# The adjacency build of a four-layer graph network, its three-lap loop written out on four engines

## The chip, the cores and the metric

The kernel runs on one core of one Trainium2 chip. The metric is the device time of one execution in microseconds. The kernel before takes 2465.7 us, the median of three runs (2464.94 to 2465.91).

## The reference

A graph of 6,250 nodes with 128 features and 206,250 directed edges (each of 100,000 random edges both ways, and a loop at each node) passes through four layers. Each layer normalizes the rows, applies a ReLU, sums over the edges and adds the result to `x`:

```
h = relu(layernorm(x)); x = x + segment_sum(edge_weight * (sigmoid(h @ Wg + bg) * (h @ W0))[dst], src)   # layer 0
h = relu(layernorm(x)); x = x + segment_sum(h[src], dst) @ W1.T + b1                                     # layer 1
h = relu(layernorm(x)); x = x + [h, segment_sum([h[src], h[dst]] @ Wm + bm)] @ Wu + bu                   # layer 2
h = relu(layernorm(x)); x = x + relu(batchnorm(D^-1 A (B^-1 A^T (h @ W3)) + b3))                          # layer 3
```

The same edge list serves all layers, so the sums over edges are products with a dense matrix of edge counts (layers 1 to 3) and of edge weights (layer 0).

## The kernel before

The 6,250 nodes lie in 49 tiles of 128. The program has three stages.

The **preparation** (up to about 100 us) loads the edges, groups them by destination, and computes layer 0's gated rows `G`.

The **build** (about 100 to 1190 us) makes the matrices, one destination tile at a time; a tile takes some 21.7 us. Four engines work on it, each with its own instruction stream, joined by semaphores alone:

- VectorE (DVE; `build` at L1059 with `hots` at L1030): for each of 8 steps h of a tile it makes one-hot rows (L1043, L1044), multiplies one set by the edge weights (L1046, which raises `hot_ready`), and adds a finished partial sum into `X` (`add_some`, L1057, which raises `added`).
- TensorE (PE; `build` at L747): for each h it waits for `hot_ready` (L751), then does two half windows (`half_windows`, L711): 12 matmuls each of one-hot rows into PSUM (L732 to L734), one matmul that takes the rounded high part away (L709), and in some of them two turns of a block (L725). Then it does a share of layer 0's sum for a pair of tiles built earlier (`sum_some`, L701 to L703). The sum of a pair starts in the first step of the next odd tile, behind the waits of `loaded` (L737), which hold until the pair's weight matrices have been turned by the DMA engines and have landed in `wt`.
- ScalarE (ACT; `build` at L1331) rounds the high parts out of PSUM (L1348, `hi_done`), the low parts (L1329, `lo_done`) and the turned blocks (L1358).
- SyncE's queue (SP; `hand_on`, L468) waits until the sums have freed a home in `wt` (`sum_made`, L477 to L480), then for `hi_done`; it loads the gated rows `g_in` (L486), issues two DMA transposes `wt<-stage` (L489), stores the counts (L493), waits for `lo_done`, loads `g_in` again and issues two more transposes. Every two tiles it loads the next edge group `meta` (L475).

So there is a ring: PE's sums of the pair of tiles before wait for transposes of that pair, and SP's transposes wait for what ACT and PE made of the current tile. Two tiles are one **pair** in the text below: an even tile and the odd one behind it.

The **passes** (about 1235 to 2440 us) multiply the counts with the rows, four times over all 49 tiles (L804), with the counts streamed from HBM. Each engine runs each pass as a loop as well.

All these loops come from one helper, `tiles_loop` (L145). It writes out the first 13 tiles (0 to 12), then opens a hardware loop of three laps with twelve tiles in its body (tiles 13 to 24, 25 to 36, 37 to 48), then writes out a drain of `lag` more steps. In the loop the tile number `j` is a register expression, so a wait such as `pe.wait_ge(s("hot_ready"), j * TILE_HOTS + (h + 1))` needs register arithmetic ahead of it; in the written-out part it is a constant. The build calls it on four engines, at L496 (SP), L764 (PE), L1087 (DVE) and L1363 (ACT).

Of the kernel before, what the change touches and what calls it, by code (L numbers as in the profile page):

```python
# [21 lines left out]
TILES = -(-NODES // P)  # L22
# [22 lines left out]
CHUNKS = -(-EDGES // P)  # L45
PADDED = CHUNKS * P
PLANES = 4
CODE = 1.0 / 64.0
RECORD = 5 * ALIGN // 2
X_PARTS = (range(0, 13), range(13, 25), range(25, 37), range(37, TILES))  # L50
# [6 lines left out]
SLOTS = 6  # L57
LAP = 2 * SLOTS
# [83 lines left out]
    return (c // 2 + 2) % (SLOTS // 2)  # L142


def tiles_loop(eng, body, lag):  # L145

    peel = LAP + 1
    for j in range(peel):
        body(j, 0, j)
    with eng.Fori(0, (TILES - peel) // LAP) as k:  # L150
        for u in range(LAP):
            body(k * LAP + (peel + u), k * (LAP // SLOTS), peel + u)
    for j in range(TILES, TILES + lag):
        body(j, 0, j)


# [45 lines left out]
def gnn_kernel(nc, x, src, dst, edge_weight, w0, wg0, bg0, w1, b1, wm, bm, wu, bu, hyper, w3, b3, gamma, beta, out):  # L202
    ctx = ExitStack()
    with ctx:
        sems = {}

        def s(name):
            if name not in sems:
                sems[name] = ctx.enter_context(nc.semaphore(name))
            return sems[name]  # L210
# [3 lines left out]
        def at(name, shape, dt, offset):  # L214
            size = int(np.prod(shape[1:])) * ESIZE[dt]
            return nc.alloc_sbuf_tensor_at(name, shape, dt, offset=offset), offset + -(-size // 32) * 32
# [73 lines left out]
        src_low, _ = at("src_low", [P, RUN], I32, o)  # L290
        pre, o = at("pre", [P, 2, BATCH, PLANES, P], F16, o)
        src_high, _ = at("src_high", [P, RUN], I32, o)
        turned, o = at("turned", [P, 2, BATCH, PLANES, P], F16, o)
        w_run, o = at("w_run", [P, RUN], F32, o)
# [92 lines left out]
        def _(sp):  # L387
# [63 lines left out]
            def layers(general):  # L451
# [41 lines left out]
                    sp.dma_start(two_tiles(j), stage[:, b, 0:FULL].rearrange("p (i a) d -> p i (a d)", a=2)).then_inc(s(f"stored{b}"), 16)  # L493
                    turn(1, "lo_done", f"lo_turned{b}")

                tiles_loop(sp, hand_on, 0)  # L496
                for a in range(WEIGHTS):
                    first = FULL + a * TILES + TURN_FIRST
                    sp.dma_start_transpose(wt[:, home(TILES - 1, 1), a, len(BY_DMA[1]):len(HALF_TILES[1])],
# [143 lines left out]
        def _(pe):  # L643
# [43 lines left out]
            def layers(general):  # L687
# [73 lines left out]
                if general:  # L761
                    general_sum(0)
                else:
                    tiles_loop(pe, build, 0)  # L764
                    for u in (HALVES - 2, HALVES - 1):
                        pe.wait_ge(s("hi_done"), (TILES - 1) * HALVES + u + 1)
                        take_high(0, TILES - 1, u)
                    for n in (GROUPS - 2, GROUPS - 1):
                        for b in range(1 + (n < GROUPS - 1)):
                            loaded(n, b)  # L770
                        for g in range(SUMS):
                            sum_some(n, n, g, n < GROUPS - 1)
# [79 lines left out]
        def _(dve):  # L852
# [10 lines left out]
            v.tensor_scalar(before[:], diff[:], 0, None, ALU.is_gt)  # L863
            v.tensor_scalar(basef[:], basei[:], CODE, None, ALU.mult)
            v.memset(ones[:], 1.0).then_inc(s("consts"), 1)
            dve.wait_ge(s("iotas"), 5)
            v.tensor_scalar(iota_c[:], iota_c[:], CODE, None, ALU.mult)
            dve.wait_ge(s("consts"), 1)
# [91 lines left out]
            def edge_keys(m, at_step):  # L960
# [10 lines left out]
                if at_step == 1:  # L971
                    v.tensor_copy(to(3), plane(2))
                    for i, g in enumerate(lot):
                        last = v.tensor_scalar(to(1)[:, i], rec[:, g, :, 24:40].bitcast(F32), CODE, basef[:, g:g + 1], ALU.mult, ALU.add)
                    last.then_inc(s("pre"), 1)
# [51 lines left out]
            def layers(general):  # L1027
# [46 lines left out]
                if general:  # L1074
                    dve.wait_ge(s("g_iotas"), 1)
                    v.memset(rows_all[:], 0.0).then_inc(s("g_prep"), 1)
                    dve.wait_ge(s("g_prep"), 1)
                    v.tensor_scalar(rows_all[:, :, 0:P], H0[:], 1.0 / H_UP, None, ALU.mult).then_inc(s("g_rows_all"), 1)
                    general_sum(0)
                    v.tensor_tensor(X[:], X[:], acc[:, :, 0:P], ALU.add).then_inc(s("g_prep"), 1)  # L1080
                    dve.wait_ge(s("g_prep"), 2)
                    for j in range(TILES):
                        v.bn_stats(stats[:, j], X[:, j])
                else:
                    dve.wait_ge(s("g_parts"), SET)
                    v.tensor_scalar(w_h[:], w_h[:], 1.0 / LOW, None, ALU.mult)
                    tiles_loop(dve, build, 0)  # L1087
                    for g in range(SUMS - 2, SUMS):
                        add_some(GROUPS - 3, g)
                    for n in (GROUPS - 2, GROUPS - 1):  # L1090
                        for g in range(SUMS):
                            add_some(n, g)
                            if n == GROUPS - 1 and g:
                                row_stats(g - 1)
                    row_stats(SUMS - 1)
# [39 lines left out]
                for ph in (1, 2, 3, 4):  # L1135
# [112 lines left out]
                    if ph == 1 and not general:  # L1248
                        degrees(Chain(dve, s("dve_b"), c1.n), LOW)

            branch(dve, layers)


# [22 lines left out]
        def _(act):  # L1276
# [48 lines left out]
            def layers(general):  # L1325
# [34 lines left out]
                if not general:  # L1360
                    for b in range(2):
                        a.activation(stage[:, b, TILES], minus16[:], ACT.Copy, scale=0.0)
                    tiles_loop(act, build, 0)  # L1363
                    for u in (HALVES - 2, HALVES - 1):
                        act.wait_ge(s("low_left"), (TILES - 1) * HALVES + u + 1)
                        low_parts(0, TILES - 1, u)
# [93 lines left out]
```

## Time and profile before

| | before |
|---|---|
| runs, median (lowest to highest) | 2465.7 us (2464.94 to 2465.91) |
| the profiled execution: its time, its span | 2461.69 us, 2459.8 us |
| PE busy | 2293.2 us (93%) |
| PE weight loads busy | 2025.0 us (82%) |
| DVE busy | 1444.7 us (59%) |
| ACT busy | 1279.8 us (52%) |
| mean granted TensorE clock | 0.978 |
| bytes moved by DMA | 569.80 MB, 232 GB/s |
| code loads (queues of kind "instruction") | q8: 200 packets, 3.28 MB; q14: 84 packets, 0.68 MB |

The span is the time from the first to the last instruction of the profiled execution. Busy time is the sum over an engine's instructions; matmuls are pipelined, so a busy PE need not be at its peak. The profiled execution is 4.0 us shorter than the median of the runs. The packets of kind "instruction" are loads of program code into the engines' instruction stores.

### The profile page before, as it was taken

How to read it: one execution, taken by the hardware profiler on the slowest of the kernel's cores; microseconds unless marked ns; L12 is line 12 of the kernel's file. 1: busy time of each engine (PE TensorE's matmuls, PEld its weight loads, DVE VectorE, ACT ScalarE, POOL GpSimd, SP SyncE). 2: the span in 40 equal slices, each digit the busy share in tenths (PEclk: the TensorE clock that was granted, in tenths of full speed). 3: DMA queues.
4: the chain of work that ended last, by engine and by line, in shares of the span. 5: the costliest groups of instructions: out<-in, count | busy, mean ns of one | idle time of the engine just before them, and what ended most of it. 6: DMA issues, size and time to landing. Idle time of an engine off the chain costs nothing.

```text
span 2459.8 us, 72172 instructions
## 1 busy us (share of the span) xinstructions
PE 2293.2 (93%) x28669; PEld 2025.0 (82%) x28669; DVE 1444.7 (59%) x3422; ACT 1279.8 (52%) x2875; POOL 57.0 (2%) x57
## 2 busy tenths in 40 slices
PE   3689999999999989999889998999998999998997
PEld 3469898998899889988768887888887888887886
DVE  8779999998899988989643233234333111222223
ACT  3689999999899989989342222222221000011112
POOL 3500000000000000000000000000000000000000
PEclk9799999999999999999989999999999999999998
DMA  7799999999999999999989999999998999999997
GB/s 188 182 213 195 201 212 207 209 210 200 189 208 208 196 203 195 205 197 205 226 202 291 290 290 290 248 261 257 258 261 214 291 290 290 264 252 241 269 268 188
DMA packets 1528563, 569.80 MB, mean 232 GB/s; under 512 B 869815, under 2 KB 1526971, under 8 KB 1528152
## 3 DMA queue, kind: packets, MB, share of 16 engines
q1 hardware_dynamic: 1524709, 559.04, 104.0%
q0 software_dynamic: 1200, 4.10, 0.6%
q8 instruction: 200, 3.28, 0.5%
q10 hardware_dynamic: 2370, 2.71, 0.4%
q14 instruction: 84, 0.68, 0.1%
HBM read 257.85 MB, written 92.19 MB: 142 GB/s over the span
## 4 chain that ended last, share of the span: by engine, by line
PE 63%; SPq 16%; ACT 9%; DMA 5%; issue 4%; DVE 3%; POOLq 1%; another core or an unknown queue 0%; POOL 0%; DVEq 0%; ACTq 0%
PE ps L804 35%; SPq L542 8%; SPq L489 5%; ACT stage L1348 4%; PE ps L732 4%; ACT stage L1329 3%; PE ps L733 3%; PE ps L734 3%; PE ps L701 3%; PE ps L702 3%; PE ps L703 3%; PE ps L709 3%; DMA wt<-stage 3%; SPq L486 2%; PE ps L725 1%
## 5 line engine op out<-in xcount | busy, mean ns | idle before, releaser
L1348 ACT CAST stage<-ps 128x784 f16<-128x784 f32 x784 | 657.4, 838 | 18.0 <-PE ps L734 10.5
L804 PE MATMUL ps<-Ha,a_tiles 128*128 128x258 f16 x4606 | 523.9, 273 | 7.2 <-DVE Ha L1124 7.2
L732 PE MATMUL ps<-hot_c,hot_r 128*128 128x98 f16 x3136 | 502.7, 210 | 13.5 <-DVE hot_c L1046 10.4
L804 PEld LDWEIGHTS ps<-Ha,a_tiles 128*128 128x128 f16 x4606 | 449.9, 98 | 73.5 <-DVE Ha L1124 7.6
L733 PE MATMUL ps<-hot_c,hot_r 128*128 128x98 f16 x3136 | 500.4, 210 | 0.0
L734 PE MATMUL ps<-hot_c,hot_r 128*128 128x98 f16 x3136 | 498.8, 209 | 0.0
L701 PE MATMUL ps<-g_in,wt 128*128 128x128 f16 x2401 | 426.9, 220 | 29.2 <-DMA wt<-stage 20.1
L1329 ACT CAST stage<-ps 128x392 f16<-128x392 f32 x784 | 405.1, 517 | 43.4 <-PE ps L709 40.8
L703 PE MATMUL ps<-g_in,wt 128*128 128x128 f16 x2401 | 426.9, 220 | 0.0
L702 PE MATMUL ps<-g_in,wt 128*128 128x128 f16 x2401 | 426.9, 220 | 0.0
L1046 DVE TENSOR_TENSOR hot_c<-hot_c,meta 128x1568 f16<-128x1568 f16 x392 | 379.2, 967 | 0.0
L732 PEld LDWEIGHTS ps<-hot_c,hot_r 128*128 128x128 f16 x3136 | 307.3, 98 | 42.3 <-ACT stage L1329 21.8
L733 PEld LDWEIGHTS ps<-hot_c,hot_r 128*128 128x128 f16 x3136 | 308.2, 98 | 13.9 <-issue 1.1
L734 PEld LDWEIGHTS ps<-hot_c,hot_r 128*128 128x128 f16 x3136 | 308.3, 98 | 0.0
L1057 DVE SCALAR_TENSOR_TENSOR X<-ps,X 128x384 f32<-128x384 f32 (+1 forms) x400 | 226.1, 565 | 111.5 <-PE ps L703 100.6
L804 PE MATMUL ps<-Hb,a_turned 128*128 128x258 f16 x2401 | 277.9, 274 | 12.6 <-DMA a_turned<-counts_by_source 10.5
L804 PE MATMUL ps<-Hb,a_tiles 128*128 128x258 f16 x2401 | 277.8, 274 | 6.9 <-DVE Hb L1124 6.9
L804 PEld LDWEIGHTS ps<-Hb,a_turned 128*128 128x128 f16 x2401 | 233.5, 98 | 50.1 <-DMA a_turned<-counts_by_source 13.6
L709 PE MATMUL ps<-stage,minus 128*128 128x392 f16 x784 | 259.5, 331 | 16.3 <-DVE hot_c L1046 9.7
L804 PEld LDWEIGHTS ps<-Hb,a_tiles 128*128 128x128 f16 x2401 | 234.9, 98 | 47.5 <-DVE Hb L1124 7.1
L1044 DVE TENSOR_TENSOR hot_r<-iota_r,meta 128x1024 f16<-128x1024 f16 x392 | 268.5, 685 | 0.0
L701 PEld LDWEIGHTS ps<-g_in,wt 128*128 128x128 f16 x2401 | 236.6, 99 | 34.4 <-issue 23.8
(199 smaller groups left out, 2338.6 us busy)
## 6 DMA issues: line engine op xcount, KB each, us to landing
a_tiles<-counts_by_source SPq DMA_DIRECT2D x147, 1600.0 KB, 13.2
counts_by_source<-stage SPq DMA_DIRECT2D x49, 1600.0 KB, 8.7
meta<-edge_groups SPq DMA_DIRECT2D x26, 128.0 KB, 2.4
wt<-stage SPq DMA_TRANSPOSE x198, 6.2
gated_parts<-G SPq DMA_DIRECT2D x7, 448.0 KB, 5.4
g_in<-gated_parts SPq DMA_DIRECT2D x98, 32.0 KB, 6.0
out_x<-X SPq DMA_DIRECT2D x12, 256.0 KB
edge_table<-tab ACTq DMA_DIRECT2D x1, 2040.0 KB, 10.6
```

Source lines behind the costliest of these rows:

```text
L701: mm(o, at_[:, 0], g_in[:, c % 4, 0:P], start=i == tiles.start and b == 0, stop=False, skip_group_check=True)
L702: mm(o, at_[:, 0], g_in[:, c % 4, P:2 * P], start=False, stop=False, skip_group_check=True)
L703: last = mm(o, at_[:, 1], g_in[:, c % 4, 0:P], start=False, stop=True, skip_group_check=True)
L709: mm(o, minus16[:], stage[:, b, FULL:FULL + TILES, u * SET_COLS:(u + 1) * SET_COLS], start=False, stop=True, skip_group_check=True).then_i ...
L732: mm(into(0), rows_, codes(0), start=v == 0, stop=True, skip_group_check=True)
L733: mm(into(1), rows_, codes(1), start=v == 0, stop=False, skip_group_check=True)
L734: last = mm(into(1), rows_, codes(2), start=False, stop=True, skip_group_check=True)
L804: last = mm(ps[:, sum_bank(ph, j, c), 0:PARTS], a_slot(ph, c, i), moving[:, i], start=i == 0, stop=i == TILES - 1)
L1044: v.tensor_tensor(hot_r[:, b], iota_r[:].unsqueeze(1).to_broadcast([P, PAIRS, P, 2]), key(0, P), ALU.is_equal)
L1046: v.tensor_tensor(hot_c[:, b, :, 1:1 + WEIGHTS], hot_c[:, b, :, 0].unsqueeze(2).to_broadcast([P, PAIRS, WEIGHTS, WCOLS, 2]), weights[:, at ...
L1329: a.copy(stage[:, b, FULL + TILES:PARTED, u * SET_COLS:(u + 1) * SET_COLS], of).then_inc(s("lo_done"), 1)
L1348: a.copy(stage[:, b, 0:2 * FULL].rearrange("p (k i) d -> p k i d", k=2)[:, :, 0:TILES, u * SET_COLS:(u + 1) * SET_COLS], of).then_inc(s("h ...
```

## The change

`tiles_loop` gets a fourth argument: how many of the last tiles to write out instead of putting them in the loop. The build passes 36 of it on all four engines, so no lap is left and no loop is opened: tiles 0 to 48 are straight code with constant tile numbers. The four passes call it without the argument and keep their loops. No arithmetic, buffer, wait or transfer is added, left out or given another order.

```diff
+WRITTEN_OUT = 36
...
-def tiles_loop(eng, body, lag):
+def tiles_loop(eng, body, lag, written_out=0):
 
     peel = LAP + 1
     for j in range(peel):
         body(j, 0, j)
-    with eng.Fori(0, (TILES - peel) // LAP) as k:
-        for u in range(LAP):
-            body(k * LAP + (peel + u), k * (LAP // SLOTS), peel + u)
-    for j in range(TILES, TILES + lag):
+    laps = (TILES - peel - written_out) // LAP
+    if laps:
+        with eng.Fori(0, laps) as k:
+            for u in range(LAP):
+                body(k * LAP + (peel + u), k * (LAP // SLOTS), peel + u)
+    for j in range(TILES - written_out, TILES + lag):
         body(j, 0, j)
...
-                tiles_loop(sp, hand_on, 0)
+                tiles_loop(sp, hand_on, 0, WRITTEN_OUT)
...
-                    tiles_loop(pe, build, 0)
+                    tiles_loop(pe, build, 0, WRITTEN_OUT)
...
-                    tiles_loop(dve, build, 0)
+                    tiles_loop(dve, build, 0, WRITTEN_OUT)
...
-                    tiles_loop(act, build, 0)
+                    tiles_loop(act, build, 0, WRITTEN_OUT)
```

Where this lands in the streams. On PE, before, tile 13 opens the loop body; the rows are PE's instructions in program order, with the semaphores each waits for (ISA and REGISTER_ALU are register arithmetic):

```order
L703 MATMUL ps<-g_in,wt 128x128
L150 UNCONDITIONAL_BRANCH
L150 ISA
L716 ISA [waits hot_ready]
L709 MATMUL ps<-stage,minus_51 128x392 [waits hi_done]
L719 REGISTER_ALU
L732 MATMUL ps<-hot_c,hot_r 128x49x2 [waits lo_done]
...
L742 ISA
L743 ISA [waits turned_out]
L742 ISA [waits g_loaded0,lo_turned0,hi_turned0]
L694 ISA [waits lo_turned1,g_loaded1,hi_turned1,turned_out]
L701 MATMUL ps<-g_in,wt 128x128 [waits added]
```

The same place in the change, PE's tile 13 (lines are three further down):

```order
L706 MATMUL ps<-g_in,wt 128x128
L712 MATMUL ps<-stage,minus_51 128x392 [waits hi_done,hot_ready]
L735 MATMUL ps<-hot_c,hot_r 128x49x2 [waits lo_done]
L736 MATMUL ps<-hot_c,hot_r 128x49x2
L737 MATMUL ps<-hot_c,hot_r 128x49x2
...
L704 MATMUL ps<-g_in,wt 128x128 [waits hi_turned1,turned_out,lo_turned1,g_loaded0,g_loaded1,lo_turned0,added,hi_turned0]
```

The matmuls and the semaphores they wait for are the same; the branch into the loop and the register instructions ahead of the waits are gone. At the other end of the body, before, PE's last rows of tiles 24, 36 and 48:

```order
L701 MATMUL ps<-g_in,wt 128x128
L702 MATMUL ps<-g_in,wt 128x128
L703 MATMUL ps<-g_in,wt 128x128
L150 REGISTER_ALU
L150 COMPARE_AND_BRANCH
```

In the change no L153 branch (where the branch's line now stands) is in the build on any engine. On SP, before, an odd tile in the body reads:

```order
L475 ISA [waits hot_ready]
L475 DMA meta<-edge_groups 128x512
L478 ISA
L485 ISA [waits sum_made]
L486 ISA [waits hi_done]
L486 DMA g_in<-gated_parts 128x128
L489 DMA_TRANSPOSE wt<-stage 128x24x128
L489 DMA_TRANSPOSE wt<-stage 128x17x128
L493 ISA
L493 DMA counts_by_source<-stage 128x25x256
```

and in the change:

```order
L478 DMA meta<-edge_groups 128x512 [waits hot_ready]
L489 DMA g_in<-gated_parts 128x128 [waits hi_done,sum_made]
L492 DMA_TRANSPOSE wt<-stage 128x24x128
L492 DMA_TRANSPOSE wt<-stage 128x17x128
L496 DMA counts_by_source<-stage 128x25x256
```

The transfers and their order are the same, without the register instructions between them.

The built program counts, for PE's twelve tiles of a lap: 4,452 matmuls (each a weight load and a multiply), 114 wait instructions, 398 register and branch instructions before; 4,452 matmuls and 215 wait instructions in the change. DVE's body has 776 instructions for twelve tiles before and 485 in the change, ACT's 813 and 599.

## Rows read from the trace of the kernel before

**Rows 1.** The page: span, busy shares, the queues that load code.

```profile
span 2459.8 us, 72172 instructions
PE 2293.2 (93%) x28669; PEld 2025.0 (82%) x28669; DVE 1444.7 (59%) x3422; ACT 1279.8 (52%) x2875; POOL 57.0 (2%) x57
...
q8 instruction: 200, 3.28, 0.5%
```

**Rows 2.** Busy time by pair of tiles (start:end, length, busy (x instructions), clock, DMA share, GB/s).

```profile
189.80:233.30 43.50, 42.82 (x743) 39.18 (x743) 40.35 (x65) 41.52 (x80) 0.00 (x0) 1.00 1.06 207
...
276.80:320.80 44.00, 42.89 (x744) 39.20 (x742) 40.44 (x65) 41.56 (x80) 0.00 (x0) 1.00 1.10 206
320.80:363.70 42.90, 42.80 (x744) 39.25 (x744) 40.32 (x65) 41.54 (x80) 0.00 (x0) 1.00 1.09 207
...
494.20:537.50 43.30, 43.08 (x743) 39.33 (x742) 40.36 (x65) 41.59 (x80) 0.00 (x0) 1.00 1.05 210
537.50:582.30 44.80, 43.13 (x744) 39.36 (x742) 40.41 (x65) 41.59 (x80) 0.00 (x0) 1.00 1.02 203
...
627.10:676.90 49.80, 44.58 (x743) 40.73 (x742) 40.28 (x65) 41.67 (x80) 0.00 (x0) 0.97 1.03 183
...
896.60:946.10 49.50, 44.68 (x743) 40.87 (x743) 40.31 (x65) 41.67 (x80) 0.00 (x0) 0.97 1.02 184
...
1033.30:1078.60 45.30, 43.13 (x744) 39.36 (x744) 40.42 (x65) 41.59 (x81) 0.00 (x0) 1.00 1.00 202
...
1123.50:1168.10 44.60, 43.15 (x743) 39.39 (x742) 40.38 (x65) 41.60 (x80) 0.00 (x0) 1.00 1.04 202
```

**Rows 3.** Line L150 from 640 to 930 us: count, min/median/max ns, first and last start.

```profile
L150 DVEq COMPARE_BRANCH  x2: 62/64/67, 642.7 to 912.2; - x2
L150 ACTq COMPARE_BRANCH  x2: 53/56/58, 646.9 to 916.4; - x2
L150 PEldq COMPARE_BRANCH  x2: 5437/5630/5824, 647.0 to 916.5; - x2
```

**Rows 4.** First work behind the first back edge, timeline by engine: start, length, operation, idle.

```profile
653.12 0.51 PE L709 MATMUL ps<-stage,minus 128*128 128x392 f16 x1 [5.06 <-DVE hot_c L1046]
...
648.24 0.57 DVE L1043 TENSOR_TENSOR hot_c<-iota_c,meta 128x784 f16<-128x784 f16 x1 [5.10 <-issue]
```

**Rows 5.** The 4 us behind the first back edge's gap, columns as in rows 2.

```profile
653.00:657.00 4.00, 3.88 (x43) 3.62 (x44) 2.29 (x4) 2.50 (x4) 0.00 (x0) 0.57 1.25 202
```

**Rows 6.** Waits of PE from 407.2 to 1168.1 us: us in total, times, longest.

```profile
PE ps L701 <- DMA wt<-stage: 11.6, 9, 2.0
PE ps L709 <- DVE hot_c L1046: 9.7, 2, 5.1
```

**Rows 7.** Timeline of PE at the start of tile 21.

```profile
561.51 0.23 PE L701 MATMUL ps<-g_in,wt 128*128 128x128 f16 x1 [1.52 <-DMA wt<-stage]
```

**Rows 8.** Chain of waits around tile 21: start, length, what.

```profile
550.44 4.59 SPq L489
555.07 6.11 DMA wt<-stage
```

**Rows 9.** SP's transposes L489 from 505 to 517 us, issue to landing.

```profile
DMA to landing us min/median/max: 4.6/6.5/6.6
```

**Rows 10.** DMA queues from 559.0 to 560.2 us: packets, MB, share of 16 engines.

```profile
q8 instruction: 1, 0.02, 4.6%
```

**Rows 11.** DMA queues from 385.2 to 654.6 us, one lap.

```profile
q8 instruction: 38, 0.62, 0.9%
```

**Rows 12.** Waits of SP from 407.2 to 1168.1 us.

```profile
SPq L485 <- PE ps L703: 31.0, 28, 4.8
```

**Rows 13.** Line L150 over the whole span, PE's sequencer.

```profile
L150 PEldq COMPARE_BRANCH  x15: 76/208/5824, 647.0 to 2433.7; - x15
```

**Rows 14.** SP's transposes L489 from 632 to 655 us, issue to landing.

```profile
DMA to landing us min/median/max: 5.1/7.7/8.9
```

## The prediction

> **What bounds the kernel now.** I read the page first: PE is busy for 93% of the span [rows 1], so what counts is where PE stands still, and for the change only in the build. Then I cut the build into pairs of tiles and read each one's length beside PE's busy time [rows 2]. The reader is to see three kinds of pair. Pairs of written-out code (tiles 4 to 11, 189.8 to 363.7 us, four pairs) last 43.5, 43.5, 44.0 and 42.9 us, mean 43.48, with PE busy for 42.8. Of the 17 pairs of tiles 14 to 47, 15 lie inside a lap; PE is busy for 43.1 to 43.2 us in them, and they last either 43.3 to 43.7 (eight, 494.20 is one) or 44.6 to 45.3 (seven, 537.50 and 1123.50 are two; mean 44.84). And the two pairs with a back edge in them last 49.8 and 49.5 us.
>
> The third view is the loop's own line: the taken branch holds PE's sequencer for 5.8 and 5.4 us, while on DVE and ACT the branch instruction itself shows 0.06 us [rows 3]. DVE nevertheless does nothing for 5.10 us behind its branch, with nothing but its own issue to wait for, and PE's first matmul of the next lap comes 5.06 us late [rows 4]. That wait is put down to DVE's `hot_c`, but PE's own branch, from 647.0 to 652.8, covers the whole gap. The granted clock is 0.57 in the 4 us behind it [rows 5]: most of them at 1.2 GHz instead of 2.4, after PE had idled.
>
> The fourth view is PE's waits in the 17 pairs of tiles 14 to 47: 9.7 us at the back edges, and 11.6 us, in nine waits, for the transposes that turn the weights [rows 6]. So the ring of PE, ACT and SP has nearly no slack in it: PE is as long as the DMA's chain to within half a microsecond. At tile 21 PE waits 1.52 us [rows 7]; the chain there ends in a transpose that lands 6.11 us after its issue began [rows 8], where the same step two tiles earlier took 4.6 [rows 9]. In just that moment one 16 KB load of PE's code goes through the same DMA engines [rows 10]. I read the long pairs as that collision: code loads come one after the other as PE walks its code, 38 in a lap [rows 11], about six per pair, and where one falls on the end of the pair's last transpose, the pair costs 1.5 us more.
>
> **The change part by part.** Tiles 0 to 12, the preparation and the passes keep their code. The stretch that changes is 407.2 to 1168.1 us, 17 pairs in 760.9 us, with half a pair more at tile 13 and tile 48 behind it.
>
> *The two back edges taken* go. Their pairs are 49.8 + 49.5 - 2 x 43.3 = 12.7 us longer than the shortest pair of a lap [rows 2]. Of each 6.4, about 4.9 is the idle time [rows 6] and the rest the slow clock. The third branch, at the end, is not taken and costs nothing that shows.
>
> *Register instructions* ahead of waits go. PE's busy time per pair is 43.08 to 43.20 in laps and 42.80 to 42.89 in written-out code [rows 2]: 0.3 us per pair, 17.5 pairs, 5 us if nothing takes their place. DVE and ACT lose theirs too, beside PE's work, and are worth nothing: ACT, the busier, has 41.6 us of work in a quiet pair [rows 2]. SP loses some 9 per pair; it stands still for 31.0 us over the 17 pairs waiting for PE's sums [rows 12], so that is worth nothing by itself.
>
> *What comes back.* The DMA chain does not get shorter. Written-out pairs show it: PE is busy 42.83 but the mean pair is 43.48, so 0.65 us is waited for per pair, against 0.2 to 0.4 in a quiet pair of a lap. So half of the register gain returns as a wait. This needs no estimate: the four written-out pairs already have the code of the change, and I take their mean, 43.48, for a quiet pair.
>
> *The collisions* stay, at other pairs. 38 loads for the 9,416 instructions of a lap is one in about 250; a pair has 1,569 of them before and 1,520 written out, by the built program's counts, and the loads are 16.4 KB each [rows 1]. If a load is 256 instructions (an estimate from those numbers), a pair is 6.13 loads before, and the place of a load moves by 33 instructions from pair to pair: it meets the transpose's end in two or three neighbouring pairs of a lap, and then is past it. That fits: the long pairs stand next to each other (537.5 and 582.3; 807.1 and 851.8; 1033.3, 1078.6, 1123.5). Written out, a pair is 5.94 loads; the place moves by 16 instructions, the other way, half as fast. In 17 pairs it goes once round, and is at the bad place in five to seven pairs in a row, by the waits' positions roughly tiles 21 to 33. I take six pairs, at 44.7 us: the chain sets their length, so a faster PE shortens little of the 44.84.
>
> Sum: 6 x 44.7 + 11 x 43.48 = 746.5 us against 760.9: 14.4 less. Tile 13 and tile 48 give 0.3 each at most, of which I take 0.3. So **about 15 us less**. In the profiled execution that is a span of 2459.8 - 14.7 = 2445; its time of 2461.69 would be 2447. The median of the runs is 4.0 above it and I carry the difference over: 2465.7 - 15 = 2450.7, written as 2450.5.
>
> The passes: their fifteen branches on PE (three per loop, five loops) have a median of 0.21 us [rows 13], so a back edge into a short loop is cheap, and they are kept. The one cost they could see is that their code lies elsewhere; by the built program each pass's loop fills no more code pages on PE or DVE than before, so I put it at nothing, bounds -1 to +2 us.
>
> The bounds of the sum: with no collision and the shortest written-out pair, 17 x 42.9 = 729.3, 31.6 less. With the dearer half of what is known, eleven collisions, 11 x 44.7 + 6 x 43.48 = 752.6, 8 less.
>
> A rule to weigh. The trace prices the branch that jumps back a long way at 5.4 to 5.8 us [rows 3]. The Trainium skill, Advanced Engine Details and Errata, Control Flow Timing, gives a compare-and-branch about 108 ns; by that the three branches would be worth 0.3 us, which is rival C's time.
>
> **The rivals.**
>
> *A. No collisions in straight code.* The seven long pairs may belong to the loop: tiles 4 to 11 are straight and have none. Then every pair costs 43.48: 739.2, 21.7 less, about 2444. Against it: those are four pairs, and by the count of instructions a load is not due there. The Trainium skill, Runtime: NRT & Kernel Launch, Instruction fetch mechanics, says that crossing a block of straight code is mostly hidden; by that A would be the time, and the trace disagrees where a load and a long transpose coincide [rows 7 to 10].
>
> *B. The chain takes everything.* PE's saved time brings each pair to the length of the colliding ones, 44.84: 762.3, 1.4 more, about 2467. For it: three pairs in a row in the last lap are at 44.6 to 45.3. Against it: the written-out pairs.
>
> *C. The stall is not the branch's.* Code must be loaded anyway, and straight code stands still for it as well, 5 us every twelve tiles. Then only the register time is won, about 2 us: 2464. Against it: the written-out tiles 0 to 12 are as much code as a lap and have no such gap in the four pairs of [rows 2].
>
> *D. Slower: two loads on one pair.* At the first back edge a burst of code loads meets the transposes, and they take up to 8.9 us to land [rows 14] instead of 6.6 [rows 9], 2.3 us more. If straight code on four engines brings PE's load and another engine's together on the chain's end, a colliding pair of 44.8 costs 2.3 more, 47.1. The even point is a mean of 760.9 / 17 = 44.76 us per pair, six such pairs beside eleven quiet ones; ten of them give 775.4, 14.5 more, 2480. Against it: DVE and ACT have fewer instructions per tile to load than before, 485 for 776 and 599 for 813.
>
> *E. The change doesn't do what it says.* The built program has no branch left in the build on any engine; I give it nothing.
>
> **How the numbers follow.** The forecast has 0.70, A 0.17, B 0.06, C 0.04, D 0.03. Range: from 2441, a few microseconds below A since quiet pairs may lie under 43.48, to 2459, which is the forecast with eleven collisions (2457) and a little for the passes. B, C and D lie outside with 0.13. A measurement of this kernel tells about 0.2%, 4.9 us, from no change. Forecast and A lie beyond that with nearly all their weight: faster 0.87. B, C and the rim of the forecast: same 0.10. D: slower 0.03.
>
> **What the profile after would show.** The span near 2445 us. No idle time of PE over 4 us in the build, and no granted clock under 1.00 from 200 to 1150 us. PE's busy time per pair at 42.8 to 42.9 throughout. Waits of PE for `wt<-stage` in the 17 pairs not gone but up, from 11.6 to some 16 us. Long pairs of about 44.7 us in one run somewhere between tiles 21 and 33, each with a transpose that lands some 6.1 us after issue, and a code load in it; if there are none, A is right, and if they are all long, B. The passes as long as before to 1 us. I am wrong in the large if a gap of 5 us stays in the build, or if pairs of 47 us appear.

## The result and the profile after

| | before | change |
|---|---|---|
| runs, median (lowest to highest) | 2465.8 us (2464.94 to 2469.34), 4 runs | 2443.8 us (2441.67 to 2447.87), 4 runs |
| the profiled execution: its time, its span | 2461.69, 2459.8 us | 2443.28, 2441.5 us |
| PE busy | 2293.2 us | 2283.5 us |
| mean granted TensorE clock | 0.978 | 0.980 |
| tiles 14 to 47, 17 pairs | 761.0 us | 744.6 us |

The ratio is 0.991, with a 95% interval of 0.9893 to 0.9927: faster by about 0.9%, which is small but clear of the scatter. Forecast were 2450.5 us and a range of 2441 to 2459; the median lies in the range, 6.7 us below the forecast. The gain is 22.0 us here and 15.6 us in a second measurement (change_again below); 15 were forecast.

The page of the change: busy time, and the queues that load code.

```profile
span 2441.5 us, 69457 instructions
PE 2283.5 (94%) x28669; PEld 2018.2 (83%) x28669; DVE 1445.4 (59%) x3422; ACT 1278.2 (52%) x2875; POOL 53.5 (2%) x57
...
q8 instruction: 191, 3.13, 0.5%
q14 instruction: 66, 0.54, 0.1%
```

The trace has 2,715 instructions fewer: 3,648 register and branch instructions are gone, on all engines together, and 933 instructions that only wait have come, where a wait stands by itself. 191 blocks of PE's code are loaded instead of 200 [rows 1].

Busy time by pair of tiles, of the change, columns as in [rows 2]. The pairs begin at tiles 4, 14, 16, 18, 20, 22, 24, 26, 28, 30, 32 and 46.

```profile
186.90:229.70 42.80, 42.70 (x744) 39.16 (x744) 40.32 (x65) 41.45 (x80) 0.00 (x0) 1.00 1.07 208
...
404.40:447.50 43.10, 42.83 (x744) 39.20 (x742) 40.39 (x65) 41.55 (x80) 0.00 (x0) 1.00 1.12 203
447.50:491.90 44.40, 42.85 (x744) 39.19 (x742) 40.40 (x65) 41.52 (x80) 0.00 (x0) 1.00 1.14 211
491.90:536.40 44.50, 42.96 (x745) 39.26 (x744) 40.49 (x65) 41.53 (x80) 0.00 (x0) 1.00 1.10 198
536.40:580.70 44.30, 42.79 (x743) 39.16 (x742) 40.34 (x65) 41.55 (x80) 0.00 (x0) 1.00 1.13 208
580.70:625.30 44.60, 42.91 (x745) 39.23 (x744) 40.46 (x65) 41.52 (x80) 0.00 (x0) 1.00 1.04 202
625.30:669.30 44.00, 42.87 (x744) 39.22 (x744) 40.42 (x65) 41.52 (x80) 0.00 (x0) 1.00 1.08 205
669.30:713.40 44.10, 42.82 (x744) 39.18 (x743) 40.38 (x65) 41.53 (x80) 0.00 (x0) 1.00 1.06 205
713.40:759.80 46.40, 44.41 (x744) 40.55 (x744) 40.41 (x65) 41.62 (x80) 0.00 (x0) 0.96 0.99 195
759.80:802.60 42.80, 42.70 (x744) 39.17 (x744) 40.30 (x65) 41.45 (x80) 0.00 (x0) 1.00 1.07 206
802.60:846.20 43.60, 42.88 (x744) 39.18 (x744) 40.31 (x65) 41.44 (x80) 0.00 (x0) 1.00 1.04 209
...
1105.30:1149.00 43.70, 42.79 (x743) 39.17 (x742) 40.34 (x65) 41.53 (x80) 0.00 (x0) 1.00 1.11 207
```

The pairs of 49.8 and 49.5 us are gone, and the seven long pairs are there still, now one behind the other at tiles 16 to 29. The last of them is 46.4 us: the clock fell in it.

```profile
736.00:740.00 4.00, 2.41 (x28) 2.26 (x29) 1.78 (x4) 1.46 (x3) 0.00 (x0) 0.78 1.20 189
740.00:744.00 4.00, 4.00 (x61) 3.74 (x59) 2.73 (x6) 2.92 (x6) 0.00 (x0) 0.79 1.02 217
```

At 0.78 and 0.79 PE spent part of these 8 us at 1.2 GHz, behind its wait of 1.89 us at tile 29. The waits of PE in the 17 pairs, where before stood [rows 6]:

```profile
PE ps L704 <- DMA g_in<-gated_parts: 11.1, 11, 1.9
PE ps L704 <- DMA wt<-stage: 1.2, 1, 1.2
PE ps L735 <- ACT stage L1332: 0.6, 1, 0.6
```

The 9.7 us at the back edges are gone, and 12.3 us of waits for the weights' chain stay. They were 11.6 before, and the prediction had them rise to some 16. The name has gone from `wt` to `g_in`, but the landing is the same moment: both are loaded for the same matmul, and at tile 23 the transpose landed at 604.28 us, `g_in` at 604.45, and the matmul began at 604.62.

The versions that the experiments below made stand here together, their pairs sorted by kind. A pair is "long" from 43.9 us; the pairs are cut at PE's own counts, so they are exact to 0.01 us. "Edge" is a pair with a back edge of PE in it; the two pairs of pe_alone_out in which the other engines' back edges fall are counted as long. "Behind tile 48" is the time from the end of tile 47 to the end of the span.

| version | median (lowest to highest) us | ratio to before, 95% | 17 pairs | quiet, mean | long, mean | behind tile 48 |
|---|---|---|---|---|---|---|
| before | 2465.8 | | 761.0 | 8, 43.47 | 7, 44.84; 2 edges, 99.3 together | 1291.7 |
| the change | 2443.8 | 0.9893 to 0.9927 | 744.6 | 10, 43.24 | 7, 44.60 | 1292.4 |
| pe_in_laps | 2458.21 (2451.19 to 2460.56) | 0.9983 to 1.0002 | 755.8 | 9, 43.27 | 6, 44.49; 2 edges, 99.4 | 1290.3 |
| pe_alone_out | 2448.31 (2445.16 to 2452.16) | 0.9937 to 0.9971 | 749.3 | 10, 43.48 | 7, 44.92 | 1291.7 |
| regs_kept | 2444.72 (2444.35 to 2447.68) | 0.9914 to 0.9957 | 747.2 | 9, 43.34 | 8, 44.65 | 1294.0 |
| shift_128 | 2446.69 (2441.62 to 2454.23) | 0.9933 to 0.9964 | 743.6 | 10, 43.09 | 7, 44.66 | 1292.6 |
| pad_pair | 2431.99 (2431.86 to 2434.18) | 0.9871 to 0.9900 | 733.5 | 17, 43.14 | none | 1293.2 |
| pad_bad | 2456.11 (2451.72 to 2461.33) | 0.9976 to 0.9996 | 753.4 | none | 17, 44.32 | 1289.8 |
| sp_in_laps | 2448.81 (2444.77 to 2455.76) | 0.9943 to 0.9970 | 744.3 | 8, 43.22 | 9, 44.29 | 1292.3 |
| all_out | 2452.39 (2449.85 to 2456.4) | 0.9956 to 0.9980 | 742.0 | 10, 43.11 | 7, 44.41 | 1303.5 |
| change_again | 2445.12 (2442.0 to 2446.36) | 0.9924 to 0.9952 | 743.5 | 11, 43.36 | 6, 44.43 | 1292.7 |
| pad_again | 2430.88 (2428.99 to 2431.77) | 0.9865 to 0.9895 | 733.3 | 17, 43.14 | none | 1292.6 |
| shift_256 | 2443.25 (2441.91 to 2445.92) | 0.9920 to 0.9951 | 745.0 | 10, 43.24 | 7, 44.65 | 1291.5 |
| three_passes_out | 2444.51 (2441.63 to 2444.99) | 0.9919 to 0.9946 | 743.3 | 10, 43.19 | 7, 44.49 | 1292.8 |

The kernel before took 2465.8 us beside the first measurement of the change, and 2460.03, 2459.54 and 2460.69 us beside the three groups of runs that followed (the first four, the next four and the last four behind the change in the table). Expectations that name a time were written against 2465.7; so ratios and pairs are compared, not times across groups. A ratio times 2465.7 us then stands beside such an expectation. Read so, two of the first eight versions missed it: sp_in_laps (2454.9, for 2441 to 2447) and all_out (2457.8, for 2441 to 2447). A third, regs_kept (2449.9, for 2445 to 2449), did something other than meant.

The pairs are those of one profiled execution of each version, and it is not always a middling one. That of pe_in_laps, 2451.19 us, is the fastest of ten; that of sp_in_laps, 2444.77 us, the fastest of six.

### The profile page after: what moved, and what is told of

Same layout as the page of the kernel before. It is cut to its first block, busy times and chain, and to the rows that moved or that the text cites. A ratio compares the mean times of both kernels' runs of the same rounds, so it can differ in the third digit from the quotient of the medians.

```text
span 2441.5 us, 69457 instructions
## 1 busy us (share of the span) xinstructions
PE 2283.5 (94%) x28669; PEld 2018.2 (83%) x28669; DVE 1445.4 (59%) x3422; ACT 1278.2 (52%) x2875; POOL 53.5 (2%) x57
## 4 chain that ended last, share of the span: by engine, by line
PE 67%; SPq 11%; ACT 10%; DMA 6%; DVE 3%; issue 2%; POOLq 0%; POOL 0%; DVEq 0%; ACTq 0%
PE ps L807 35%; SPq L545 8%; PE ps L735 4%; PE ps L704 4%; PE ps L736 4%; PE ps L737 4%; ACT stage L1351 4%; PE ps L706 4%; PE ps L705 4%; ACT stage L1332 4%; PE ps L712 3%; SPq L492 2%; ACT wt L1361 2%; DMA a_turned<-counts_by_source 2%; PE ps L728 2%
## 5 line engine op out<-in xcount | busy, mean ns | idle before, releaser
L807 PE MATMUL ps<-Hb,a_turned 128*128 128x258 f16 x2401 | 279.5, 275 | 12.9 <-DMA a_turned<-counts_by_source 10.9
## 6 DMA issues: line engine op xcount, KB each, us to landing
a_tiles<-counts_by_source SPq DMA_DIRECT2D x147, 1600.0 KB, 12.3
```

The source lines that it names most:

```text
L807: last = mm(ps[:, sum_bank(ph, j, c), 0:PARTS], a_slot(ph, c, i), moving[:, i], start=i == 0, stop=i == TILES - 1)
```

## The experiments

Edits are shown against the change.

**One engine in laps (pe_in_laps).** Which engine's back edge costs the 5 us?

```diff
-                    tiles_loop(pe, build, 0, WRITTEN_OUT)
+                    tiles_loop(pe, build, 0)
```

> PE's build goes back into the loop of three laps; SP, DVE and ACT stay written out. Theory (PE's own taken branch holds it for 5.4 to 5.8 us): both gaps of about 5 us stay in PE's stream, with the slow clock behind them, and PE's register work stays; 2464 to 2466 us, the time before. Rival (the gap is DVE's, as the wait is put down to DVE's hot_c): the gaps go, 2448 to 2452 us.

Measured: 0.9993 of before. The waits of PE from 404 to 1160 us, and its sequencer on the loop's line:

```profile
PE ps L704 <- DMA wt<-stage: 10.8, 9, 2.1
PE ps L712 <- issue: 9.6, 2, 5.2
```

```profile
L153 PEldq COMPARE_BRANCH  x2: 5148/5582/6017, 641.6 to 909.8; - x2
```

No other engine has a branch in the build now, so PE's own accounts for the whole gap, and the profile says so: "issue" stands where it named DVE's `hot_c` in [rows 6]. The two pairs with an edge take 99.4 us, as before. The quiet pairs are as short as the change's, 43.27, though PE executes 1,124 register instructions in the 17 pairs and none in the change: **PE's register work costs nothing that shows in this trace.** The trace is of the fastest of the ten executions, 7 us below their median; where the others lost these 7 us no trace tells.

**PE alone written out (pe_alone_out).**

```diff
-                tiles_loop(sp, hand_on, 0, WRITTEN_OUT)
+                tiles_loop(sp, hand_on, 0)
...
-                    tiles_loop(dve, build, 0, WRITTEN_OUT)
+                    tiles_loop(dve, build, 0)
...
-                    tiles_loop(act, build, 0, WRITTEN_OUT)
+                    tiles_loop(act, build, 0)
```

> Only PE's build is written out; SP, DVE and ACT are in laps. Theory: each engine has a stall of its own at its back edge, and they lie over one another; ACT's runs from 648.0 to 652.9 us in the trace before, and PE needs ACT's output at once, so about 4 us of each gap stays, put down to ACT, and DVE's costs 2 us or less behind it. PE's register work goes. 2453 to 2459 us. Rival (only PE's branch counts): 2443 to 2446 us, the change's time.

PE's waits from 404 to 1160 us, and two pairs of this version (one quiet, one with the others' back edge):

```profile
PE ps L704 <- DMA g_in<-gated_parts: 7.5, 11, 1.7
PE ps L712 <- DVE hot_c L1049: 4.2, 2, 2.5
```

```profile
761.30:804.90 43.60, 43.11 (x744) 39.36 (x744) 40.41 (x65) 41.59 (x81) 0.00 (x0) 1.00 1.06 210
...
891.40:937.10 45.70, 43.06 (x743) 39.30 (x742) 39.38 (x64) 41.54 (x80) 0.00 (x0) 1.00 1.07 204
```

A gap remains at each edge, but a smaller one. At the first edge PE waits 1.72 us for DVE and, 2 us later, 0.94 us for ACT; at the second it waits 2.48 us for DVE. The pairs with them take 46.09 and 45.76 us. Expected were about 4 us for ACT, so the size and the name were off, while the ratio fits. So PE's edge is the one that counts, and beneath it lies another of about half the size, which shows when PE's alone is taken out.

And the second reading: PE has no register instruction here, yet its busy time per pair is 43.12 (before 43.14 in pairs without an edge), where pe_in_laps has 42.88 and the change 42.84. The 0.26 us that the prediction gave to PE's registers belong to the other engines. PE's weight loads show where. Their waits in the 17 pairs, of before, of pe_alone_out, of pe_in_laps and of the change:

```profile
PEld ps L725 <- ACT stage L1329: 25.7, 102, 0.3
...
PEld ps L732 <- ACT stage L1329: 9.6, 34, 0.3
```

```profile
PEld ps L728 <- ACT stage L1332: 25.7, 102, 0.3
PEld ps L735 <- ACT stage L1332: 10.8, 35, 1.2
```

```profile
PEld ps L728 <- ACT stage L1332: 23.1, 102, 0.3
...
PEld ps L735 <- ACT stage L1332: 7.0, 34, 0.2
```

```profile
PEld ps L728 <- ACT stage L1332: 22.8, 100, 0.3
...
PEld ps L735 <- ACT stage L1332: 7.9, 35, 0.9
```

In each step PE waits 0.2 to 0.3 us for the low part that ACT rounds. With ACT's register instructions in the stream this is 35.3 and 36.5 us in the 17 pairs, without them 30.1 and 30.7: 5 us, beside 17 x 0.26 = 4.4 us of PE's busy time. SP, DVE and ACT were in laps together in both versions with the long waits. SP alone does not do it: in sp_in_laps, below, these waits are 30.3 us and PE's busy time is 42.82 per pair. That of DVE and ACT it is ACT is argued from the waits' name, not shown.

**SP in laps (sp_in_laps).**

```diff
-                tiles_loop(sp, hand_on, 0, WRITTEN_OUT)
+                tiles_loop(sp, hand_on, 0)
```

> SP's build goes back into laps; PE, DVE and ACT stay written out. SP's own branch took 0.06 us in the trace before and its next instruction came 0.3 us later. Theory: worth nothing, within 3 us of the change (2441 to 2447), with no gap over 3 us. Rival (SP's register instructions between transfers lengthen the transpose chain, of which nothing is to spare): quiet pairs at 43.3 to 43.5 us instead of 43.0, 3 to 8 us more, 2447 to 2452.

```profile
L153 SPq COMPARE_BRANCH  x2: 45/52/58, 669.3 to 930.4; - x2
```

The 17 pairs take 744.3 us, the quiet ones 43.22: in this trace SP's laps cost nothing in the build, and the rival's quiet pairs of 43.3 to 43.5 us are not there. But the time is 0.9956 of before, where the change has 0.991 and 0.9938, and it lies above both the theory and the rival. The intervals just overlap (0.9943 to 0.9970 here, 0.9924 to 0.9952 for change_again), and the profiled execution is the fastest of the six. So whether SP's laps cost the other executions some 4 us stays open.

**Laps of one (regs_kept).** Meant to keep the register arithmetic and lose the back edges.

```diff
-    for j in range(TILES - written_out, TILES + lag):
+    if written_out:
+        for lap in range(written_out // LAP):
+            with eng.Fori(0, 1) as k:
+                for u in range(LAP):
+                    c = peel + lap * LAP + u
+                    body(k * LAP + c, k * (LAP // SLOTS), c)
+    for j in range(TILES, TILES + lag):
```

> The build of all four engines as three loops of one lap each: straight code with no branch taken, but with all the register instructions. Theory: no gap over 3 us, PE busy 43.1 us per pair instead of 42.8, six or seven long pairs, at other tiles than in the change (by the count of instructions near tiles 21 to 25 and 35 to 41). The register work is worth 5 us at most, of which the waits for transposes take back a part: 2445 to 2449 us. Rival (the register work is most of the gain): 2455 to 2460 us.

The edit did not do this. Loops of one lap are built with constants: the trace has 4 register instructions per engine from 404 to 1150 us, where before has 1,102 on PE, 1,061 on DVE and 873 on ACT. So it is the change with three seams in it, at 747.2 us for the 17 pairs against 742.0 to 745.0 in five versions (the change, change_again, shift_256, three_passes_out, all_out) whose build is the change's. It says nothing on the register work, on which pe_in_laps and pe_alone_out tell.

**The place of the code loads (shift_128, shift_256).** 64 small matmuls more in the preparation, 128 of PE's instructions, then 128 of them, 256 instructions. They write a part of PSUM that is overwritten before it is read.

```diff
+            for f in range(64):
+                mm(ps[:, 5, 0:GROUPS], hot_b[:, f // 2, :, f % 2], hot_g[:, f // 2, :, f % 2], start=True, stop=True)
```

> The change, with 64 matmuls of 25 columns more on PE in the preparation, in a place where PE waits for the weights for 8 us; their output is never read. They move all later PE code by 128 instructions, half a code load of 256. Theory (a pair is long where a code load falls on the end of its last transpose): the run of long pairs at tiles 16 to 29 leaves there and comes at tiles 4 to 13 and again from tile 32 to 45, twelve long pairs instead of seven, some 6 us more: 2447 to 2453 us. Rival (the long pairs have to do with the tile or the time, not with the code's place): long pairs stay at tiles 16 to 29, 2442 to 2446 us.

> The change with 128 small matmuls more in the preparation, 256 of TensorE's instructions, one whole load of code; they write a part of PSUM that is overwritten before it is read. Theory (the place of the loads decides, and it is the same modulo 256 as in the change): the long pairs are back at tiles 16 to 29, tiles 4 to 15 and 30 to 47 are quiet but for one or two. Rival (the 64 small matmuls of shift_128 moved the long pairs by their time, or by any amount of code): long pairs stand at tiles 4 to 12 and 32 to 42, as in shift_128, or elsewhere. The build is 2 to 4 us later by the matmuls themselves; time 2440 to 2450 us.

Lengths of the pairs in us, by their first tile:

```
tile         4     10    12    14    16    20    28    30    32    36    42    44
change     42.79 43.22 43.53 43.12 44.40 44.37 46.39 42.80 43.59 42.81 43.36 43.50
shift_128  44.56 43.88 44.09 42.82 42.80 42.82 43.20 43.22 44.47 44.29 44.38 42.82
shift_256  42.79 42.95 43.30 43.56 44.22 44.42 46.45 42.80 43.39 43.05 42.83 43.20
```

Half a load of code moves the long pairs away from tiles 16 to 29 to tiles 4 to 13 and 32 to 43; a whole load brings them back to 16 to 29. So the period is 256 instructions. Two things blur the picture. The pairs of tiles 6 and 8, not in the table, last 44.08 and 43.93 us in the change already (46.48 and 44.15 in shift_128). And one pair of shift_128 stands outside the run, tile 18's with 46.67 us: there too a load began 0.53 us before the last transpose was done but for one part, that part came 1.49 us late, and behind PE's wait of 2.33 us the clock fell.

**The place held still (pad_pair, pad_bad).** Sixteen waits already fulfilled in each pair of tiles make it 1,536 of PE's instructions, six whole loads; the place no longer moves. pad_bad has besides 51 small matmuls in the preparation, which set it onto the transposes.

```diff
+PAD_PER_H = 1
...
+                        for _ in range(PAD_PER_H if j >= 4 else 0):
+                            pe.wait_ge(s("hot_ready"), j * TILE_HOTS + (h + 1))
```

> The change, with one wait more on PE per step h from tile 4 on, on a semaphore value that has been reached already: eight instructions a tile, which makes a pair 1,536 instructions, six code loads of 256 exactly. The place of a load in the pair then stays where it is at tile 5, which is a quiet one. Theory: no run of long pairs, all pairs 42.8 to 43.5 us, the seven waits of 1.0 to 1.9 us gone, some 9 us, and the slow clock behind the longest, 2 us; the added waits cost PE's sequencer 1 to 3 us. 2433 to 2439 us, faster than the change. Rival (long pairs come from contention that has no fixed place): 2444 to 2448 us.

> The same padding, and 51 matmuls more in the preparation, whose output is never read: the place of a load stays fixed in the pair, 102 instructions further, where the long pairs of the change had it. Theory: nearly every pair from tile 5 to 47 is long, 44.2 to 44.6 us, 21 pairs times 1.3 us over pad_pair, 20 to 30 us: 2456 to 2466 us. Rival: no difference from pad_pair beyond 3 us.

One pair (tiles 22 and 23) of pad_again, the same kernel as pad_pair, and one of pad_bad:

```profile
576.00:619.00 43.00, 42.88 (x744) 39.23 (x744) 40.40 (x65) 41.54 (x80) 0.00 (x0) 1.00 1.13 218
```

```profile
584.70:629.20 44.50, 42.86 (x744) 39.20 (x744) 40.43 (x65) 41.52 (x80) 0.00 (x0) 1.00 1.05 203
```

PE works 42.9 us in both, and both have the sixteen added waits, so it is not these that make the difference. PE's waits in the 17 pairs of pad_bad are 23.2 us:

```profile
PE ps L707 <- DVE hot_c L1054: 15.2, 11, 1.6
PE ps L707 <- DMA wt<-stage: 8.0, 6, 1.9
```

The name `hot_c` misleads here. In the pair above, the last transpose landed at 608.16 us and the sum's first matmul, put down to `hot_c`, began at 608.51, 0.35 us behind it, as in the rows of before and of the change below.

In the landings the reason can be read. Each of the two transposes of a tile's low part lands in 16 parts, as its semaphore events show. Worked out from the records of the landings and of the queue that loads PE's code, for the transpose that a pair's sum waits for:

```
version, tiles    load begins   15 parts landed by   16th part   sum begins
before 20, 21       559.12          559.66            561.18       561.51
change 22, 23       602.29          602.78            604.28       604.62
pad_bad 22, 23      606.10          606.64            608.16       608.51
pad_again 22, 23     none           597.63            597.64       598.30
```

"None" means: in the 5 us before the sum.

A load of code that begins some 0.5 us before the transpose is done holds up one part of 16 by 1.5 us, and the wait is for all 16. This was counted over the 34 transposes (two for each of 17 pairs) of the odd tile's low part in each of seven traces. There the last part comes over 1.2 us behind the fifteenth 9 times before, 5 times in the change, 5, 4 and 4 times in change_again, shift_128 and shift_256, 16 times in pad_bad, and never in pad_again. That is 43 times, and each time a load had begun 0.47 to 0.73 us before the fifteenth part landed, and the last part came 1.43 to 1.57 us behind it. (The other way round, a load begins that close without a late part 8 times.) In pad_again parts come late too, 6 times in the stretch, but in transposes that PE's sum does not wait for last.

Three of the change's seven long pairs, tiles 16 to 21, show no late part in this transpose; a load begins 2.6 to 3.8 us ahead of their sums, in an earlier link of the same chain. They move with the others in shift_128 and come back with them in shift_256, so they hang on the loads' place as well, but which transfer is held up there was not resolved.

**The same on one chip (change_again, pad_again).**

> This is the change itself, for a comparison on one chip. Theory (TensorE's code loads of 256 instructions meet the end of the last weight transposes): the 17 pairs of tiles 14 to 47 take 743 to 747 us, with seven long pairs of 43.9 to 46.4 us at tiles 16 to 29 and quiet ones of 42.8 to 43.8 elsewhere, as in the first profile of the change; the time is 2438 to 2447 us, 0.6 to 1.1% below the kernel before. Rival (the long pairs are a disturbance of that one execution): they stand at other tiles this time, or there are none and the 17 pairs take about 734 us.

> The change with sixteen repeated, already fulfilled waits per pair of tiles, so that a pair is 1,536 instructions, six whole loads of code. Theory: the place of a load against the transposes is the same in every pair, and a quiet one; the 17 pairs take 733 to 735 us, none but one or two over 43.9 us, and the time is 9 to 12 us below that of the change on the same chip, 2430 to 2435 us. Rival (the first measurement of this version fell on a quicker chip): less than 4 us below the change here.

Side by side, 2445.12 and 2430.88 us, 14.2 us apart where 9 to 12 were expected, and no run of the one reaches the other's. The pairs account for 10.2 of the 11.0 us between the spans (2440.2 and 2429.2). In change_again the pairs of tiles 16 to 29 are 44.37, 44.54, 44.46, 44.21, 43.87, 44.22 and 44.81 us: the same tiles as in the first profile. In change_again PE waits 11.9 us for `g_in` and 1.3 us for `wt` in its 17 pairs; in pad_again its longest waits there are these:

```profile
PE ps L705 <- DMA wt<-stage: 1.3, 4, 0.4
PE ps L705 <- issue: 1.2, 5, 0.4
```

**The padded change is the best version**: 0.988 of before (0.9865 to 0.9895), in a first measurement 0.9885.

**The passes written out too (all_out, three_passes_out).** In three_passes_out pass 4 keeps its laps.

```diff
-                        tiles_loop(pe, step, 2)
+                        tiles_loop(pe, step, 2, 0 if general or ph == 4 else WRITTEN_OUT)
```

and so on SP, DVE and ACT; all_out has it without `ph == 4`.

> The change, with the four passes written out on four engines as well. Their back edges took PE 0.21 us each in the trace before, eight taken. Theory: PE runs from an own chain of matmuls there and neither branches nor registers bound it, worth 0 to 2 us; more code loads run beside the streams of counts, each pass about 15 more on PE, which may cost as much: 2441 to 2447 us, no difference from the change. Rival (code loads collide with the streams as in the build): 2448 to 2460.

> The change with the first three passes written out as well; only the fourth keeps its laps. Theory (in all_out it is the fourth pass, whose loads of code meet the DMA transposes of a_turned, that lost 11 us): the part behind tile 48 takes 1290 to 1295 us, as in the change, and the time is within 3 us of the change's. Rival (straight code costs in every pass): the part behind tile 48 is 1298 to 1303 us, the time 6 to 10 us above the change's.

Queue and wait, of all_out and then of three_passes_out:

```profile
q8 instruction: 231, 3.78, 0.6%
...
PE ps L807 <- DMA a_turned<-counts_by_source: 24.8, 19, 2.0
```

```profile
q8 instruction: 221, 3.62, 0.6%
...
PE ps L807 <- DMA a_turned<-counts_by_source: 13.5, 14, 1.9
```

The wait is 10.9 us in the change. The expectation for all_out, no difference, failed; its rival held. Passes 1 to 3 load 30 blocks of code more and lose nothing (1292.8 us behind tile 48, 1292.4 in the change); pass 4 adds 10 blocks and loses 10.7 us, nearly all of it in waits for the transposes `a_turned`. That the loads hold these up as they do in the build is likely but was not tried by moving them. The rival in three_passes_out, straight code costing in every pass, is refuted.

## Why the prediction came out right, point by point

**The back edges**: right, and of the right size. Against two quiet pairs of before they were worth 99.3 - 2 x 43.47 = 12.4 us (12.7 taken). PE's own branch makes the gap, as the prediction read it, and the cheap branch that it weighed against this, 0.3 us for all three, is refuted. Rival C, the same stall in straight code, is refuted: no such gap is left in the change.

**The register work**: the amount was right, 0.26 us of PE's busy time per pair (0.3 taken); its place was wrong. The step failed was "DVE and ACT lose theirs too, beside PE's work, and are worth nothing". It is theirs that shows, and PE's that does not. The reason given, that ACT has 41.6 us of work in a pair of 43, looked at a sum, where each step holds a short wait of PE for ACT. SP's loss was miscounted, too: by the traces it has 103 instructions fewer in twelve tiles, 17 per pair and not 9. Nothing in the sum rests on that.

**What comes back**: the mean of four written-out pairs, 43.48, stood for a quiet pair; measured are 43.24, with 42.8 in the shortest. This is the term that was mis-sized: ten quiet pairs by 0.24 are 2.4 us. The four pairs have waits of their own (1.01 us in the pair of tile 8 before, 0.99 in the change) that the later ones do not have.

**The collisions**: the mechanism was right, and the count nearly. Six long pairs at 44.7 were taken, seven at 44.60 found, in one run, with the place of a load moving half as fast as before; they begin at tile 16, not 21. Four of the seven show the late part that the prediction described, three do not. With 7 x 44.60 + 10 x 43.24 the stretch is 744.6; the forecast had 746.5.

**The clock**: not foreseen. It adds about 1.5 us to PE's busy time in one pair (44.41 for 42.86) of the change, shift_256 and regs_kept, and in two pairs of shift_128. "No granted clock under 1.00" was wrong at one place.

**Outside the stretch**: behind tile 48, 0.7 us more, inside the bounds for the passes. Tile 14 begins 2.8 us sooner, at 404.4 for 407.2, in code that is unchanged. In other versions with the same start it begins from 403.2 to 406.4, so this looks like scatter between executions, with one profile of before to judge by. The forecast was 2445 us for the span, measured are 2441.5: 1.9 of the 3.5 lie in the pairs, the rest mainly here. And the profiled execution was 0.5 us below the median this time, not 4.0, which makes the other 3.5 us or so of the 6.7. Carrying the 4.0 over was a guess that did not hold: the kernel before itself had medians of 2459.5 to 2460.7 us beside the later runs.

**How much of the hit was luck.** The two large terms, the edges and the collisions, were right by their mechanism. The register work hit its amount with the wrong engines. The quiet pairs were taken 2.4 us too long in total; a seventh long pair, 1.1 us more than the quiet one in whose place it stands, offset part of that, and 1.5 us of the long pairs' time are the slow clock, which was not foreseen. And the lower bound of the sum, 31.6 us less, lay outside the stated range; pad_pair, with all pairs quiet, has 733.5 us for the 17 pairs against the 729.3 of that bound.

**The rivals.** A named almost the measured time, 2444, for a wrong reason: it had no collisions and 43.48 for each pair. The seven long pairs, their moving with 128 instructions and their return with 256 refute it. So does the padding: without collisions the kernel is at 2431. The Trainium skill, Runtime: NRT & Kernel Launch, Instruction fetch mechanics, holds the crossing of a code block to be mostly hidden. For PE's own stream the traces agree: 101 blocks were loaded in the 17 pairs of the change, and PE's waits there are all put down to the weights' chain or ACT (the three rows above), none to its own issue. It does not cover the load as a transfer, and that is where the 1.5 us come from. B is refuted by ten quiet pairs. D is refuted as a forecast: in no version does PE stand still for more than 2.33 us in a pair without a back edge. But its even point is real: pad_bad, with all 17 pairs long, gives back nearly everything, 0.9986 of before (0.9976 to 0.9996).

## What to carry to other kernels

Read a loop's back edge on the engine that bounds the kernel: here 5 to 6 us each, where SP's branch took 0.05. After writing code out, look whether long steps come in runs that drift from step to step; then count the engine's instructions per step, and make them a whole number of code loads (256 for PE here) with a few harmless instructions, at a place where no awaited transfer ends: that gave 14 us after the change's 15 to 22. Before writing out a loop whose engine waits for DMA transposes, look for a gain to set against the loads: pass 4 had none and lost 10.7 us.

## What the runs showed of the hardware that was not expected

- A load of 16 KB of PE's code held up one of the sixteen parts of a DMA transpose by 1.43 to 1.57 us in each of the 43 late landings counted; the other fifteen had landed by then.
- After a wait of 1.89 us at tile 29 the granted clock fell to 0.78 for 8 us in the change, while change_again waited 1.85 us at the same tile and lost no clock (busy time 42.85). The length of the wait alone does not decide it: before waited 2.02 us at tile 43 and kept a granted clock of 1.00, shift_128 waited 2.00 us at tile 7 and lost it.
- With DVE and ACT in laps, register instructions in their streams, PE's busy time was 0.26 us per pair longer, in waits of its weight loads of 0.2 to 0.3 us; PE's own laps left no trace in it.
